# Attention's value matmuls in two halves of 256 query columns, on either side of the second score pair

## What is computed

```python
sc = (-jnp.einsum('bhqi,bhki->bhqk', q[..., :1], k[..., :1]) + jnp.einsum('bhqc,bhkc->bhqk', q[..., 1:], k[..., 1:])) / dh ** 0.5
at = jax.nn.softmax(sc, axis=-1)
out = jnp.einsum('bhqk,bhkc->bhqc', at, vv)
```

## Time and profile before

| | us |
|---|---|
| median of 3 runs (2517.89 to 2521.94) | 2518.19 |
| profiled execution, its time | 2521.54 |
| its span in the trace | 2519.6 |
| the exps, first to last start | 757.1 to 1726.1 |
| PE, ACT, DVE busy over the span | 2157.1, 1461.7, 1188.3 |

### The profile page before, as it was taken

One profiled execution on the slowest core, in us unless ns is written; L12 is line 12 of the kernel. 1 busy time (PEld: TensorE's weight loads), 2 busy tenths in 40 slices (PEclk: granted clock), 3 DMA queues, 4 the chain that ended last, 5 costly groups with the idle time before them and its releaser, 6 DMA issues. The chain is left out here.

```text
span 2519.6 us, 40347 instructions
## 1 busy us (share of the span) xinstructions
PE 2157.1 (86%) x12472; PEld 1032.1 (41%) x12473; DVE 1188.3 (47%) x2471; ACT 1461.7 (58%) x2353; POOL 384.4 (15%) x630
## 2 busy tenths in 40 slices
PE   5987899924969999999999999999258999999992
PEld 4786455513631222222222222225135666666662
DVE  5567322256883444444444444311774444444444
ACT  2216333325749999999999999997442222222220
POOL 0030466640000000000000000000002222222220
PEclk9998899966979999999999999999678999999996
DMA  5001222251100000000000000004364444334445
GB/s 186 1 1 68 70 77 79 75 196 44 35 5 1 1 1 1 1 1 1 1 1 1 1 1 1 1 1 119 107 176 121 123 120 118 117 118 122 120 118 209
DMA packets 106479, 160.29 MB, mean 64 GB/s; under 512 B 10488, under 2 KB 82928, under 8 KB 106352
## 3 DMA queue, kind: packets, MB, share of 16 engines
q1 hardware_dynamic: 91568, 117.18, 15.2%
q0 software_dynamic: 13632, 37.24, 4.5%
q10 hardware_dynamic: 1152, 4.19, 0.4%
HBM read 118.86 MB, written 35.39 MB: 61 GB/s over the span
## 5 line engine op out<-in xcount | busy, mean ns | idle before, releaser
L1675 ACT ACTIVATE at_pexp<-at_psS 128x1024 f32<-128x1024 f32 x1024 | 959.5, 1022 | 40.3 <-PE at_psS L1578 39.4
L1592 PE MATMUL at_psO<-at_pexp,at_vst 128*32 128x512 f32 x4096 | 547.0, 606 | 0.1
L1689 DVE TENSOR_REDUCE at_mx<-at_psM 128x2 f32<-128x1024 f32 x237 | 290.1, 1224 | 494.9 <-PE at_psM L1605 494.9
L1578 PE MATMUL at_psS<-l1c_QT,l1c_KT 64*128 64x512 f16 x2048 | 399.7, 387 | 54.0 <-ACT at_pexp L1675 44.2
L1578 PEld LDWEIGHTS at_psS<-l1c_QT,l1c_KT 64*128 64x128 f16 x2048 | 98.4, 92 | 645.4 <-ACT at_pexp L1675 624.3
L1996 PE MATMUL ex_psH<-wide_wgu,ex_xT 128*128 x852 | 340.2, 549 | 0.1
L2040 ACT ACTIVATE ex_sg<-ex_bias 128x228 f32<-128x228 f32 x213 | 83.7, 393 | 288.4 <-DVE ex_bias L2066 288.4
L2066 DVE TENSOR_TENSOR ex_bias<-ex_psH,ex_bias 128x456 f32<-128x456 f32 x213 | 134.7, 633 | 195.7 <-PE ex_psH L1996 194.7
L1996 PEld LDWEIGHTS ex_psH<-wide_wgu,ex_xT 128*128 128x128 f32 x852 | 157.3, 191 | 138.6 <-issue 138.6
L982 POOL DMA_INDIRECT expert_rows<-ex_y,ex_odx x142 | 140.8, 991 | 396.5 <-issue 285.8
L2019 PE MATMUL ex_psY<-wide_w2b,ex_hT 114*128 (+1 forms) x852 | 196.0, 379 | 0.7 <-DVE ex_y L2085 0.7
(11 more groups left out here) (339 smaller groups left out, 2470.1 us busy)
## 6 DMA issues: line engine op xcount, KB each, us to landing
ex_bias<-in_L_ffn_bg SPq DMA_DIRECT2D x71, 342.0 KB, 4.7
ex_bias<-in_L_ffn_b SPq DMA_DIRECT2D x71, 342.0 KB, 5.1
normed<-rt_area SPq DMA_DIRECT2D x16, 512.0 KB, 2.6
lm_y<-expert_rows SPq DMA_DIRECT2D x16, 512.0 KB
cb_y<-expert_rows SPq DMA_DIRECT2D x16, 512.0 KB, 9.4
l_w<-in_L_ffn_w SPq DMA_DIRECT2D x24, 256.0 KB
wide_wgu<-in_L_ffn_Wg SPq DMA_DIRECT2D x8, 684.0 KB
wide_wgu<-in_L_ffn_W SPq DMA_DIRECT2D x8, 684.0 KB
```

Source lines behind the costliest of these rows:

```text
L1578: mm = pe.matmul(psS[:, n, hh * BANK:(hh + 1) * BANK], keys(k.KT, p)[r, kt * P:(kt + 1) * P], keys(k.QT, p)[r, c * BANK:(c + 1) * BANK], s ...
L1592: mm = pe.matmul(psO[g * VW:(g + 1) * VW, y, :], vst[:, p % 2, hh, kt, :], pexp[:, (p * ST + step) % 3 * 2 + n, hh * BANK:(hh + 1) * BANK] ...
L1675: act.activation(pexp[:, u % 6, :], psS[:, u % 2, :], ACT.Exp, scale=D ** -0.5 / (QS * QS)).then_inc(raised, 1)
L1689: dve.tensor_reduce(mx[:, 2 * t:2 * t + 2], psM[:, :, :], AX.X, ALU.max).then_inc(reduced, 2)
```

## The change

A weigh is made in two calls, each on half of the query columns (256 of 512): the first stands where the whole stood, between n0 and n1; the second behind n1 (and behind `means`, ahead of `turn_out` and `turn_shift`). Each call again makes four matmuls with the same weights. The weighs of key blocks 0 and 15 (steps 0, 1, 30 and 31 of a pair, made in steps 2, 3, 0 and 1) stay whole. `weighed` goes up by 1 for each half, and ScalarE's wait is rewritten for it.

```diff
-                def weigh(p, step):
+                def weigh(p, step, half):
                     kt, y = step // 2, step % 2
+                    w, wide = half * (BANK // 2), BANK // (1 if whole(step) else 2)
...
                     for g in range(4):
                         n, hh = g // 2, g % 2
-                        mm = pe.matmul(psO[g * VW:(g + 1) * VW, y, :], vst[:, p % 2, hh, kt, :],
-                                       pexp[:, (p * ST + step) % 3 * 2 + n, hh * BANK:(hh + 1) * BANK],
+                        at = hh * BANK + w
+                        mm = pe.matmul(psO[g * VW:(g + 1) * VW, y, w:w + wide], vst[:, p % 2, hh, kt, :],
+                                       pexp[:, (p * ST + step) % 3 * 2 + n, at:at + wide],
                                        start=(kt == 0), stop=(kt == KT16 - 1))
-                    mm.then_inc(weighed, 2)
+                    mm.then_inc(weighed, 2 if whole(step) else 1)
+
+                def whole(step):
+                    return step // 2 in (0, KT16 - 1)
+
+                def behind(p, step, half):
+                    p, step = (p, step - 2) if step >= 2 else (p - 1, ST - 2 + step)
+                    if p >= 0 and not (half and whole(step)):
+                        weigh(p, step, half)
...
                         scores(p, step, 0)
-                        if step >= 2:
-                            weigh(p, step - 2)
-                        elif p:
-                            weigh(p - 1, ST - 2 + step)
+                        behind(p, step, 0)
                         scores(p, step, 1)
                         q, n = mean_at(p, step)
                         if q < NPAIR and step % 2 == 0:
                             means(q, n // 2, turns_by(p, step))
+                        behind(p, step, 1)
                         if step in (3, 5) and p:
                             turn_out(p - 1, step // 4)
...
-                    act.wait_ge(weighed, u + 1)
+                    act.wait_ge(weighed, u // 2 * 2 + 2)
```

More of the change, by code:

```diff
@@ L1661, in _ @@
                             turn_shift(p + 1)
-                weigh(NPAIR - 1, ST - 2)
-                weigh(NPAIR - 1, ST - 1)
+                weigh(NPAIR - 1, ST - 2, 0)
+                weigh(NPAIR - 1, ST - 1, 0)
                 for y in range(2):
```

## The result

| | before | after |
|---|---|---|
| median | 2518.4 us (2517.9 to 2521.9, 5 runs) | 2531.0 us (2529.5 to 2533.1, 5 runs) |
| ratio | | 1.0049, 95% interval 1.0034 to 1.0063 |
| span of the profiled execution | 2519.6 us | 2527.5 us |

The account below looks back on a forecast made before the run. A latency loop through the whole weigh bound the kernel, then TensorE: 14 pairs +16.4 us, first pair +0.6, last pair -1.3, pair 15's end -0.5, sum +15.2, taken as +16 on 2518.2: 2534 us, range 2521 to 2547.

Parts of the forecast that it names:

- The loop of 3.74 us: Before the change, exp, n0, whole weigh, n1 and next exp close a latency loop that sets two steps at 3.74 us.
- The price of a half: Half a weigh takes 0.57 us, not 0.50; each additional block costs TensorE 0.25 us, score pairs 0.890 apart.
- TensorE becomes the bound: In split steps TensorE needs 3.785 us per two steps, above ScalarE's 3.65 and the former 3.742; given 0.70.
- One sign: In the changed kernel's trace, ScalarE shows short idle times ahead of an exp, one in two steps, released by the scores.
- Means to half: The step from the means to the second half, absent from the trace, taken as 0.32 us, bounds 0.21 and 0.35.
- The wait in steps 1 and 2: Whole steps at a pair's start, where TensorE runs ahead and waits for ScalarE: 0.4 to 0.5 us lost.
- the turning of the shift: Between n1 and n0 once in a pair: 0.68 us less its entry, so 0.36 charged to TensorE.
- the sum over a pair: TensorE's starts, 61.20 us, plus its waits make 61.7 a pair against 60.53 before, 1.17 more.
- The last pair: Without means, TensorE's 3.56 us is under ScalarE's pace; two steps fall from 3.74 to 3.65, saving 1.3 us.
- (a): Rival on the halves: block overhead mostly hidden, a half at 0.50 us, ScalarE's pace reached, 2491 us; chance 0.10.
- (d): Rival on the halves: weight loads or means to half cost 0.025 us more each, another 20 us, 2554; chance 0.12.
- (b): Rival on a pair: no wait in steps 1 and 2, halves 10 ns less, 60.6 us, about 2520; chance 0.08.

Follow-up runs that it names:

- the 240-column run: The changed kernel with 240 instead of 256 columns in each half, the other 32 query columns of key blocks 1 to 14 left out: 2507.8 us, ratio 0.9962.
- the fastest kernel: Against the kernel before, three weigh blocks in two steps from step 6, the third behind n1 of the odd step, finishing that weigh and starting the next: ratio 0.9954.

## Why the prediction was right

Forecast was 2534, +16; measured 2531.0, +12.6.

- **The bound before.** The loop of 3.74 us through the whole weigh was read rightly: one whole weigh left in two steps keeps it, 32 columns less lower it by 0.053, to 3.69.
- **The price of a half.** 0.57 us, and stretches of 0.890: measured 0.57 (1200.28 to 1200.85) and 0.89. The reading of the overhead from two rows of unlike column counts was the step that decided the sign; proportion (0.50) would have given the rival's gain. The Trainium skill's page "TensorEngine Tiling (Array Packing)", "Key Properties", says that a change of the tiling mode drains TensorE; the run with both halves together agrees: there, four more matmuls without a further change of tiling cost under 0.01 us. The same page of the Trainium skill gives each matmul an overhead of about 60 cycles ("Instruction Overhead"); that doesn't show in this run, where 16 records take the 1.00 us of 8.
- **TensorE becomes the bound.** 3.785 computed, 3.78 measured, no wait left in the middle of a pair, clock 1.00; the 240-column run gave 23 us back for four times 0.027 us in two steps. One sign did not come out as written: ScalarE shows no idle time there. The exp of the odd step's n0 does start late, 1.05 us after the one before (1202.23 to 1203.28) and 0.43 after its scores, but the one before lasts just as long.
- **Means to half** took 0.31 (1201.97 to 1202.28), 0.32 was taken.
- **The wait in steps 1 and 2** was computed at 0.4 to 0.5. The row is n0 of step 2; n1 of step 1 starts at 1187.97, 0.67 before it, where 0.21 would do:

```profile
1188.64 0.39 PE L1578 MATMUL at_psS<-l1c_QT,l1c_KT 64*128 64x512 f16 x2 [0.29 <-ACT at_pexp L1683]
```

- **The term that was mis-sized** is the turning of the shift in the sum over a pair. I charged 0.36 us from the 0.68 of the earlier trace rows, as if TensorE had been busy all that time. After the change:

```profile
1667.29 0.64 PE L1594 MATMUL at_psO<-at_pexp,at_vst 128*32 128x256 f32 x8
1667.75 0.22 PE L1637 MATMUL at_psM<-top_identh,at_shift 128*32 128x128 f16 x1
1667.90 0.39 PE L1578 MATMUL at_psS<-l1c_QT,l1c_KT 64*128 64x512 f16 x2
```

  From the half to n0 it is 0.61 instead of 0.57, so the turning costs 0.04. The row offers the reason: it is a 128*32 matmul, of the same tiling as the half in front of it; no run tested that by itself. The 0.32 too much are nearly all of the difference between 61.7 and the measured 61.35 a pair, and over 14 pairs 4.5 of my 16 us. Without them the sum is +11, beside the 10.0 by which the stage grew. The medians' +12.6 lies nearer to the forecast than the stage does, and that is luck: the rest of the kernel, which the change doesn't touch, differs by 2 us between the two profiled executions alone.
- **The last pair** became faster, as said: its 49 exps behind the last late one are (45.02 - 1.02) / 48 = 0.917 apart, against 0.937 in the earlier trace rows.

```profile
1687.50 45.02 ACT L1683 ACTIVATE at_pexp<-at_psS 128x1024 f32<-128x1024 f32 x49 [0.37 <-PE at_psS L1578]
```

- **The rivals.** Cheaper halves (a) and dearer ones (d) are refuted by the 0.57, the tie (b) by the 0.8 us a pair. A slip in the range: a half dearer by 13 ns is 11 us, so the upper end should have been 2545 and not 2547.

## What to carry to other kernels

An engine that is 99% busy need not be the bound: divide a long merged row by its count and compare with the shortest interval, and look for the loop that closes over two engines and the number of buffers between them. When work is cut to shorten such a loop, price the additional entries and exits from rows with different sizes, and add up the other engine's starts; and check not one stretch but every run of neighbouring stretches against the pace. Here, with two places for scores, the score pair two units on can start its exp 1.50 us after the exp it waited for began, and two exps take 1.83: TensorE may fall behind by only 0.3 us. And when work is moved from one stretch to another, ask whether some longer loop holds both: its sum doesn't change.

## What was new about the hardware

- Cutting a set of four 32-column float32 matmuls in two, side by side in the queue, costs nothing visible (1.00 us for 8 records of 512 columns and for 16 of 256). Leaving the 64*128 score tiling for one block in 128*32 and coming back costs 0.25 us: 0.10 at the entry, some 0.02 in the first pass, 0.12 at the exit.
- A small matmul (128 columns, float16) cost 0.04 us beside work of its own tiling.
- An exp of 128 x 1024 can follow the one before it at 0.92 us or less though it lasts 1.02 to 1.05 us. In the fastest kernel exps that last 1.03 are followed at 0.90, so the length doesn't delay the next exp; it delays what waits for the end, the 0.02 us in the loop there.
